# One kernel of causal attention and expert layers: its attention stage and its expert stage put into one program, with two orders of work inside changed

## The chip, the cores and the metric

The kernel runs on one NeuronCore of a Trainium2 chip. The metric is the device time of one execution in microseconds (us), as the median of several runs. The engines named here are TensorE (PE, with PEld for its weight loads), VectorE (DVE), ScalarE (ACT), GpSimd (POOL) and SyncE (SP), which issues most DMAs.

## The reference

A transformer layer over 4096 tokens of width 256 in float32: attention and a feed-forward part with experts both read the same normalised input, and both are added to x.

```python
xn = _layernorm(x)
# attention: 16 heads of 16, causal, over all 4096 tokens
Q, K, V = (heads(xn @ w) for w in (W_Q, W_K, W_V))
probs = softmax(Q @ K.T / 4 + causal)
att = (probs @ V).reshape(B, S, 256) @ W_o
# experts: 16 of them, each takes the C = 512 tokens that score highest for it
scores = softmax(flat_x @ gate_w.T).T
topk_weight, topk_idx = top_k(scores, C)
xg = flat_x[topk_idx]                                   # [16, 512, 256]
h = gelu(xg @ Wg.T) * (xg @ Wu.T)                       # [16, 512, 1024]
eo = (h @ Wd.T) * topk_weight[..., None]
out = zeros_like(flat_x).at[topk_idx].add(eo)
shared = (gelu(xn @ Sg.T) * (xn @ Su.T)) @ Sd.T         # inner width 512
return x + att + out + shared
```

## The kernel before

The program has three blocks. A block is a stretch in which every engine runs its own list of instructions; at its end all engines wait for one another. The first block makes small constants. The second holds the projections (`project`) and the attention (`attend`). The third (`experts`) first runs `mix`, which for 8 groups of 512 tokens computes the output projection of attention and the shared expert and adds x, and then the 16 routed experts in a loop of 8 turns of two.

**Attention.** There are 32 tiles: 4 groups of 4 heads by 8 stretches of 512 queries. For each tile the row maxima of the scores come first ("units": a product of 128 queries by up to 512 keys on PE at L1248, reduced by DVE at L1075). Then come the scores again, transposed and with the maximum taken off (L1337), the exponential on ACT (L1205), and the products with V (pieces, L1364). The order of all this is written out ahead by a planner as a list of rows (`STREAM`); each engine goes through it in its own way.

**Uses.** Units, maxima, the counts of the top-k search, the output rows of a tile ("out") and the late work share four PSUM banks, `a_pm0` to `a_pm3`, in turn. Each such piece of work is a use: PE fills the bank of use n only when DVE has done with use n - 4 (`eng.wait_ge(s_mf, BANKS + DONE[USES[n - BANKS]])`), and DVE counts the uses up in the order in which it does them, so that `DONE` of a use is its place in DVE's order.

**Late products.** The q and k projections of the last two token groups are not made in `project` but among the first rows of attention: two groups of four products of 128 by 512, `late_products` (L467), in rows 2 to 5 and 8 to 11. The float32 result is split in a high part, rounded by ACT (`late_high`, L486), and the rest, which DVE subtracts (`late_low`, L490). `late_low` ends the use. Both parts are then stored by SP (`late_store`). In DVE's order (`TURNS`, made by `delayed`) each late use is put off by `BEHIND = 3` uses: after a late product PE fills the other three banks, and DVE does these three first. `BEHIND` is also used by the planner to place the maximum of a tile behind three units of the next.

**The seam.** At the end of attention PE turns the last tile's rows (`use(("out", LAST))`, L1292, after ACT has copied them from PSUM, L1211), DVE divides them by their sums (L1150, L1152), SP stores them and waits for all stores. After the block's end PE begins `mix` with the turns of the first group's attention rows (`turn(0, 0)`, `turn(0, 1)`, L1600, whose inputs `k.A0` and `k.A1` were loaded during attention), opens the bank of the token lists (`lists.open_pe`, L647), and makes the gate and up products (`up`, L1588). The operand of the first group, `k.XP0`, is made by POOL during attention; that of the second group (`m_xp`) by POOL at L1493 and L1410 from a load that SP issues in `mix`.

**Experts.** For each expert PE makes gate and up products (L1888) and down products (L1898) for 8 chunks of the inner width; the results of the down products for four blocks of 128 tokens, t = 0 to 3, gather in two banks `e_po`, two blocks in each. The last chunk's product ends with `s_dn`. DVE then waits for `s_dn` and scales the four blocks by the tokens' weights (L1868), and POOL, once all four are there, adds them to the output rows with four indirect DMAs (L1763). PE may write `e_po` again when the four are scaled; it asks for that behind the next expert's first two pairs of products. `wait_alone` is a wait followed by an increment of a counter that nothing else uses.

Of the kernel before, what the change touches and what calls it, by code (L numbers as in the profile page):

```python
# [57 lines left out]
class Core:  # L58


    def __init__(self, nc, ctx):
        self.nc, self.ctx = nc, ctx
# [7 lines left out]
    def sem(self, name):  # L70
        return self.ctx.enter_context(self.nc.semaphore(name))
# [631 lines left out]
def attend(nc, k, shared, front, project):  # L703
# [14 lines left out]
    with ctx:  # L718
# [13 lines left out]
        s_kv = [front.s_kv, [c.sem(f"a_kv1{n}") for n in range(NQ)]]  # L732
        s_q = [*front.s_q, *[c.sem(f"a_sq{n}") for n in range(4, SLOTS)]]
        s_nq = [c.sem(f"a_nq{n}") for n in range(SLOTS)]
        s_one, s_pad, s_one1, s_pad1 = front.s_one, front.s_pad, c.sem("a_one1"), c.sem("a_pad1")
        s_mb, s_mf, s_nm, s_sp = (c.sem(f"a_{n}") for n in ("mb", "mf", "snm", "sp"))
        s_st, s_ex, s_pv, s_ev, s_rd = (c.sem(f"a_{n}") for n in ("st", "ex", "pv", "ev", "srd"))
        s_as = [c.sem(f"a_as{n}") for n in range(2)]
        s_shd, s_ws, s_wh, s_wl = (c.sem(f"a_{n}") for n in ("shd", "sws", "wh", "wl"))
# [23 lines left out]
        LAG, BACKLOG, PAUSE, BEHIND = 2, 6 * P, 2, 3  # L763
# [206 lines left out]
        with nc.Block() as block:  # L970
            @block.sync
            def _(eng):
                def fetch_q(t):
                    front.queries(eng, QT[t % SLOTS], s_q[t % SLOTS], *TILES[t])

                def store_rows(t):
                    g, j = TILES[t]
                    eng.wait_ge(s_mf, BANKS + DONE["out", t])
                    eng.dma_start(av[:, j * NB:(j + 1) * NB, g * HG * DH:(g + 1) * HG * DH],
                                  AN[t % 2][:, :, :]).then_inc(s_as[t % 2], 16)  # L980

                project_sync(eng)
                for u in EVENTS:
                    if u[0] == "max":
                        store_max(eng, u[1])
                        if u[1] == 0:
                            front.ahead(eng, 3)
                    elif u[0] == "late":
# [9 lines left out]
                for w in range(len(WINDOWS)):  # L998
                    if w == SOFT + 8:
                        soft.sync(eng)  # L1000
# [70 lines left out]
            def _(eng):  # L1071
# [118 lines left out]
                for u in TAIL:  # L1190
                    work(u)
# [808 lines left out]
```

## Time and profile before

| | us |
|---|---|
| median of 3 runs | 2385.93 |
| lowest, highest | 2378.39, 2398.73 |
| the profiled execution | 2398.66 |
| its span, from the first to the last instruction | 2396.4 |

The profiled execution, busy time of each engine with its share of the span and the number of instructions:

```profile
PE 2320.5 (97%) x20269; PEld 1498.3 (63%) x20275; DVE 1927.1 (80%) x3721; ACT 1493.3 (62%) x2901; POOL 247.4 (10%) x239
```

And in 40 equal slices of 60 us, each digit a busy share in tenths; `PEclk` is the clock that TensorE was granted, in tenths of full speed, where 9 stands for 90% or more:

```profile
PE   7889999999999999999999999998999999999997
DVE  6766999999999999999999999975745666666664
ACT  2213677788888787878887777874224454544443
PEclk9976999999999999999999999999999999999998
```

Projection takes the first two slices, attention goes to about 1640 us, `mix` to 1834, the routed experts to 2380. A matmul on a PE at half clock takes about twice as long, so a busy share of 9 there is less work.

### The profile page before, as it was taken

Reading aid. Unit: us, or ns where it says so; the run is one execution under the profiler, and the core shown is the slowest. Engines: PE = TensorE matmul, PEld = TensorE weight load, DVE = VectorE, ACT = ScalarE, POOL = GpSimd, SP = SyncE. Lnnn points to the kernel's source line nnn. Section 1 sums busy time; section 2 is a strip of 40 time slices with the busy share of each in tenths; the row PEclk is TensorE's granted clock in tenths of the full one; section 3 lists DMA queues with packets and bytes.
Section 4 is the critical chain, followed back from the end, with each engine's and each line's share of the span. In section 5 each row is a group of like instructions: output and inputs, shape, how many; then the busy total and the mean of one; then the engine's idle time right before and its main releaser. Section 6 shows DMA issues by size and latency. Waiting matters only on the chain. (4 is left out here: it accounts for less than half of the span.)

```text
span 2396.4 us, 52700 instructions
## 1 busy us (share of the span) xinstructions
PE 2320.5 (97%) x20269; PEld 1498.3 (63%) x20275; DVE 1927.1 (80%) x3721; ACT 1493.3 (62%) x2901; POOL 247.4 (10%) x239
## 2 busy tenths in 40 slices
PE   7889999999999999999999999998999999999997
PEld 4544555455555555555555555556888888888886
DVE  6766999999999999999999999975745666666664
ACT  2213677788888787878887777874224454544443
POOL 3100000000000000000002000001130332333232
PEclk9976999999999999999999999999999999999998
DMA  7813221002100003300001000001343444444444
GB/s 257 317 54 92 57 48 37 10 11 47 40 7 11 12 19 70 62 14 12 6 11 41 4 2 4 14 23 52 106 160 118 98 136 135 122 101 136 137 110 111
DMA packets 141243, 167.98 MB, mean 70 GB/s; under 512 B 53100, under 2 KB 106860, under 8 KB 140956
## 3 DMA queue, kind: packets, MB, share of 16 engines
q1 hardware_dynamic: 126908, 141.96, 19.0%
q0 software_dynamic: 14128, 23.20, 5.3%
q8 instruction: 137, 2.24, 0.4%
q14 instruction: 70, 0.57, 0.1%
HBM read 117.86 MB, written 48.56 MB: 69 GB/s over the span
## 5 line engine op out<-in xcount | busy, mean ns | idle before, releaser
L1075 DVE TENSOR_REDUCE a_mp<-a_pm 128x1 f32<-128x512 f32 (+3 forms) x2176 | 1295.1, 664 | 88.8 <-PE a_pm L1248 47.3
L1205 ACT ACTIVATE a_p<-a_ps 128x512 f32<-128x512 f32 (+2 forms) x2176 | 1120.8, 587 | 371.8 <-PE a_ps L1337 257.2
L1364 PE MATMUL a_po<-a_p,a_v 128*32 128x384 f32 (+2 forms) x8688 | 614.1, 385 | 0.9
L1248 PE MATMUL a_pm<-a_k,a_qr 48*128 48x512 f32 (+3 forms) x1152 | 410.2, 450 | 22.6 <-DVE p_parts L490 9.1
L1248 PE MATMUL a_pm<-a_k,a_q 48*128 48x512 f32 (+3 forms) x1152 | 408.5, 436 | 4.6
L1337 PE MATMUL a_ps<-a_qr,a_k 50*128 50x512 f32 (+3 forms) x1152 | 386.0, 433 | 2.5 <-DMA a_qr<-a_nb 2.5
L1337 PE MATMUL a_ps<-a_q,a_k 50*128 50x512 f32 (+3 forms) x1152 | 372.3, 422 | 0.8 <-ACT a_p L1205 0.5
L1364 PEld LDWEIGHTS a_po<-a_p,a_v 128*32 128x32 f32 x8688 | 202.2, 109 | 201.9 <-issue 133.7
L1337 PEld LDWEIGHTS a_ps<-a_qr,a_k 50*128 50x128 f32 x1152 | 191.8, 191 | 177.0 <-ACT a_p L1205 145.1
L1337 PEld LDWEIGHTS a_ps<-a_q,a_k 50*128 50x128 f32 x1152 | 185.1, 185 | 186.4 <-ACT a_p L1205 160.8
L1806 ACT ACTIVATE e_g<-e_pg 128x512 f32<-128x512 f32 x128 | 76.5, 598 | 242.4 <-PE e_pu L1888 242.4
L1248 PEld LDWEIGHTS a_pm<-a_k,a_qr 48*128 48x128 f32 x1152 | 190.6, 192 | 55.5 <-DVE a_mp L1075 16.2
L1855 DVE TENSOR_TENSOR e_hf<-e_g,e_pu 128x512 f32<-128x512 f32 x128 | 88.1, 688 | 168.9 <-ACT e_g L1806 154.7
L1248 PEld LDWEIGHTS a_pm<-a_k,a_q 48*128 48x128 f32 x1152 | 188.0, 184 | 28.5 <-DVE a_mp L1075 21.9
L1898 PE MATMUL e_po<-e_wdp,e_hp 128*128 128x256 f32 x1536 | 203.3, 284 | 0.0
L1898 PEld LDWEIGHTS e_po<-e_wdp,e_hp 128*128 128x128 f32 x1536 | 196.5, 191 | 8.2
L1888 PE MATMUL e_pg<-a_qr,e_wgup 128*128 128x512 f32 x768 | 197.5, 392 | 0.0
L1888 PE MATMUL e_pu<-a_qr,e_wgup 128*128 128x512 f32 x768 | 194.9, 389 | 0.0
L1888 PEld LDWEIGHTS e_pu<-a_qr,e_wgup 128*128 128x128 f32 x768 | 144.2, 188 | 30.4
L1888 PEld LDWEIGHTS e_pg<-a_qr,e_wgup 128*128 128x128 f32 x768 | 138.1, 189 | 24.2
L1763 POOL DMA_INDIRECT out<-e_y,e_iy x64 | 104.0, 1624 | 270.3 <-DVE e_y L1868 255.6
L1060 POOL CAST a_k<-a_k 128x1024 fp32r<-128x1024 f32 (+1 forms) x4 | 3.7, 929 | 1099.8 <-DMA a_k<-shared 1099.6
(196 smaller groups left out, 2066.2 us busy)
## 6 DMA issues: line engine op xcount, KB each, us to landing
e_wgu<-in_wg SPq DMA_DIRECT2D x18, 1024.0 KB, 5.4
e_wgu<-in_wu SPq DMA_DIRECT2D x18, 1024.0 KB, 7.8
e_wd<-in_wd SPq DMA_DIRECT2D x18, 1024.0 KB, 10.1
a_k<-k_parts SPq DMA_DIRECT2D x58, 128.0 KB, 3.1
q_parts<-p_parts SPq DMA_DIRECT2D x14, 512.0 KB, 6.4
k_parts<-p_parts SPq DMA_DIRECT2D x14, 512.0 KB, 7.6
a_q<-q_parts SPq DMA_DIRECT2D x96, 64.0 KB, 2.4
a_qr<-q_parts SPq DMA_DIRECT2D x78, 64.0 KB, 2.3
```

What stands on the lines that cost most here:

```text
L1060: eng.tensor_copy(k.WSH[n][:, :, 0, :], k.WSH[n][:, :, 1, :].bitcast(F32)).then_inc(s_wh, 1)
L1075: eng.tensor_reduce(mp[:, i, heads[0]:heads[-1] + 1, r, kc], ps[:, 0:len(heads) * w].rearrange("p (a n) -> p a n", n=w), AX.X, ALU.max).th ...
L1205: eng.activation(pr[:, i, heads[0]:heads[-1] + 1, off:GT], pS[n % HEADS][:, 0:len(heads) * w].rearrange("p (a n) -> p a n", n=w), ACT.Exp) ...
L1248: last = eng.matmul(ps[:, n * w:(n + 1) * w], QT[t % SLOTS][tile, a, r * P:(r + 1) * P], KT[g % 2][tile, a, kc * GT:kc * GT + w], start=n ...
L1337: last = eng.matmul(ps[:, m * w:(m + 1) * w], KT[TILES[t][0] % 2][tile, a, b * P:(b + 1) * P], QT[t % SLOTS][tile, a, off:GT], start=m == ...
L1364: last = eng.matmul(pO[h * VW:(h + 1) * VW, lo:hi], V[TILES[t][0] % 2][:, b, h * VD:h * VD + VW], PR[blk % PBUF][:, h, lo:hi], start=b == ...
L1763: eng.indirect_dma_start(out=rows, out_offset=bass.IndirectOffsetOnAxis(ap=IY[s][:, t:t + 1], axis=0), in_=Y[s][t][:, :], in_offset=None, ...
L1806: eng.activation(G[ic % 2][:, :], pG[ic % 2][:, :], ACT.Gelu).then_inc(s_gl, 1)
L1855: eng.tensor_tensor(HF[ic % 2][:, :], G[ic % 2][:, :], pU[ic % 2][:, :], ALU.mult).then_inc(s_h, 1)
L1888: last = eng.matmul(ps[ic % 2][:, :], WGUP[ic][:, a, w * DC + d, :], XT[s][:, d, b, :], start=n == 0, stop=n == DC * len(PAIRS) - 1)
L1898: last = eng.matmul(pO[t // 2][:, (t % 2) * D:(t % 2 + 1) * D], HP[ic % 4][:, a, t * P:(t + 1) * P], WDP[ic][:, b, :], start=ic == n == 0 ...
```

## The change

Three things are changed.

1. The attention no longer has a block of its own. `attend` returns its five lists of instructions, and `experts` runs them in its block ahead of those of `mix`; the wait of all engines for one another at the seam is gone. The semaphores of `attend` are made to live as long as the program. PE waits instead for DVE's uses (`taken`): for all but the last before `turn(0, 0)`, then it does the last tile's rows, then `turn(0, 1)`, then it waits for DVE's last use before it opens the list bank. SP waits for `k.s_xp0` before it loads the third group's tokens over `k.XT0`.
2. In DVE's order a late use is put off by `HOLD = 1` use instead of three. `BEHIND` stays 3 where the planner uses it.
3. The routed experts' last step goes by halves: a new semaphore `s_do` is raised by the last product of token block 1, DVE starts to scale blocks 0 and 1 at it and waits for `s_dn` only before block 2. POOL waits for each scaled block by itself before its indirect DMA.

The diff without the lines that are only indented differently:

```diff
 class Core:
-        self.nc, self.ctx = nc, ctx
+        self.nc, self.ctx, self.whole = nc, ctx, ctx
     def sem(self, name):
-        return self.ctx.enter_context(self.nc.semaphore(name))
+        return self.whole.enter_context(self.nc.semaphore(name))
...
 def attend(nc, k, shared, front, project):
-        LAG, BACKLOG, PAUSE, BEHIND = 2, 6 * P, 2, 3
+        LAG, BACKLOG, PAUSE, BEHIND, HOLD = 2, 6 * P, 2, 3, 1
...
                     if u[0] == "late":
-                        held.append([u, BEHIND])
+                        held.append([u, HOLD])
...
-        with nc.Block() as block:
-            @block.sync
-            def _(eng):
+        def sync(eng):
...
-                use(("out", LAST))
+            return lambda: use(("out", LAST))
+
+        def taken(eng, before=0):
+            eng.wait_ge(s_mf, BANKS + DONE["out", LAST] - before)
+
+        assert AT["out", LAST] % BANKS
+    return sync, gpsimd, vector, scalar, tensor, taken
...
 def mix(nc, k, x, wo, sg, su, sd, out):
                     if g > 0:
                         eng.wait_ge(s_xl, g)
+                    else:
+                        eng.wait_ge(k.s_xp0, 2)
                     tokens(g + 2)
...
-            for d in range(DC):
-                turn(0, d)
+            taken(eng, 1)
+            turn(0, 0)
+            last_rows()
+            turn(0, 1)
+            taken(eng)
             lists.open_pe(eng, pI)
...
-def experts(nc, k, out, mixed):
+def experts(nc, k, out, attended, mixed):
...
+                attend_sync(eng)
                 mix_sync(eng)
...
+                attend_gpsimd(eng)
                 mix_gpsimd(eng)
...
-                        wait_alone(k, eng, s_oe, TG * (e + 1) + TG)
                         for t in range(TG):
+                            wait_alone(k, eng, s_oe, TG * e + t + 1 + TG)
                             eng.indirect_dma_start(out=rows, out_offset=bass.IndirectOffsetOnAxis(
...
+                attend_scalar(eng)
                 mix_scalar(eng, first)
...
+                attend_vector(eng)
                 mix_vector(eng, first)
...
-                        eng.wait_ge(s_dn, IC * (e + 1) + IC)
                         eng.wait_ge(s_w4, e + 1)
                         eng.wait_ge(s_add, e + 1)
                         for t in range(TG):
+                            if t == 0:
+                                eng.wait_ge(s_do, e + 1)
+                            elif t == 2:
+                                eng.wait_ge(s_dn, IC * (e + 1) + IC)
                             eng.tensor_scalar(Y[s][t][:, :], pO[t // 2][:, (t % 2) * D:(t % 2 + 1) * D],
...
+                        if ic == IC - 1 and t == 1:
+                            last.then_inc(s_do, 1)
                     last.then_inc(s_dn, 1)
...
-                mix_tensor(eng, lambda eng: turn(0, 0, 0))
+                last_rows = attend_tensor(eng)
+                mix_tensor(eng, lambda eng: turn(0, 0, 0), last_rows, taken)
```

## Rows read from the trace of the kernel before

**Rows 1.** Table of stages: stretch, length, busy PE, PEld, DVE, ACT, POOL, PEclk, DMA.

```profile
108.90:231.80 122.90, 104.85 (x545) 52.80 (x546) 73.54 (x131) 33.66 (x64) 2.47 (x5) 0.65 0.25 81
231.80:1639.70 1407.90, 1398.03 (x15006) 747.44 (x15006) 1313.34 (x2415) 1103.71 (x2152) 15.53 (x10) 1.00 0.11 25
...
1834.50:2380.20 545.70, 545.63 (x3176) 481.56 (x3174) 342.39 (x663) 273.66 (x540) 162.14 (x124) 1.00 0.47 129
```

**Rows 2.** PE's waits from 100 to 235 us: total, times, longest.

```profile
PE a_pm L1248 <- DVE p_parts L490: 9.1, 4, 2.5
PE a_pm L1248 <- DVE p_xn L490: 4.7, 2, 2.4
PE a_pm L1248 <- DVE p_x L490: 4.0, 2, 2.3
PE a_ps L1337 <- DMA a_qr<-a_nb: 2.5, 1, 2.5
```

**Rows 3.** Timeline around one late product: start, length, instructions, idle before.

```profile
158.76 1.99 PE L467 MATMUL a_pm<-p_xs,p_wqk 128*128 128x512 f32 x4
...
160.78 0.60 ACT L486 ACTIVATE p_x<-a_pm 128x512 fp32r<-128x512 f32 x1 [1.09 <-PE a_pm L467]
161.21 1.89 DVE L1075 TENSOR_REDUCE a_mp<-a_pm 128x1 f32<-128x512 f32 x3 [0.71 <-PE a_pm L1248]
163.01 0.68 DVE L490 SCALAR_TENSOR_TENSOR p_x<-a_pm,p_x 128x512 fp32r<-128x512 f32 x1
...
163.75 0.79 PE L1248 MATMUL a_pm<-a_k,a_qr 48*128 48x512 f32 x2 [2.34 <-DVE p_x L490]
...
164.58 2.96 DVE L1075 TENSOR_REDUCE a_mp<-a_pm 128x1 f32<-128x512 f32 x5 [0.89 <-PE a_pm L1248]
```

**Rows 4.** Timeline: PE's first instruction behind two other stalls.

```profile
173.58 0.53 PE L1248 MATMUL a_pm<-a_k,a_qr 48*128 48x384 f32 x2 [1.63 <-DVE p_x L490]
...
1311.29 0.49 PE L1248 MATMUL a_pm<-a_k,a_qr 48*128 48x512 f32 x1 [1.77 <-DVE a_mp L1075]
```

**Rows 5.** One microsecond each, behind these two stalls, columns as in rows 1.

```profile
174.00:175.00 1.00, 1.00 (x12) 0.99 (x11) 0.64 (x2) 0.04 (x1) 0.00 (x0) 0.50 0.19 76
...
1312.00:1313.00 1.00, 1.00 (x12) 0.46 (x5) 1.00 (x3) 0.00 (x0) 0.00 (x0) 1.00 0.00 0
```

**Rows 6.** Groups of instructions: the late products (four matmuls each), busy us, mean ns.

```profile
L467 PE MATMUL a_pm<-p_xs,p_wqk 128*128 128x512 f32 x32 | 27.2, 1000 | 0.1
```

**Rows 7.** Two stretches of attention at either clock, columns as in rows 1.

```profile
194.23:231.78 37.55, 37.55 (x250) 19.59 (x252) 23.30 (x39) 16.43 (x31) 2.47 (x5) 0.50 0.37 113
235.19:272.60 37.41, 36.92 (x377) 20.10 (x375) 36.61 (x66) 24.68 (x49) 0.00 (x0) 1.00 0.33 87
```

**Rows 8.** Timeline of the seam between attention and mix.

```profile
1640.45 0.63 PE L1292 MATMUL a_pm<-identf,a_ot 128*128 128x128 f32 x4 [0.80 <-ACT a_ot L1211]
...
1641.41 0.42 DVE L1152 TENSOR_TENSOR a_an<-a_pm,a_rd 128x256 f32<-128x256 f32 x1
...
1645.24 1.08 PE L1600 MATMUL m_pt<-identf,a_qr 128*128 128x128 f32 x4 [4.16 <-PEq L970]
...
1647.05 2.37 PE L1588 MATMUL m_pg<-a_qr,a_k 128*128 128x512 f32 x6
...
1647.88 1.04 POOL L1493 CAST m_xp<-e_wgup 128x1024 fp32r<-128x1024 f32 x1 [84.99 <-DMA e_wgup<-xn_t]
...
1649.25 1.54 PE L1588 MATMUL m_pu<-a_qr,a_k 128*128 128x512 f32 x6
...
1667.38 0.94 PE L1588 MATMUL m_pg<-m_xp,a_k 128*128 128x512 f32 x3
```

**Rows 9.** Timeline of the end of the last expert.

```profile
2375.48 4.65 PE L1898 MATMUL e_po<-e_wdp,e_hp 128*128 128x256 f32 x36
...
2380.17 1.66 DVE L1868 TENSOR_SCALAR e_y<-e_po,e_w 128x256 f32<-128x256 f32 x4 [1.46 <-PE e_po L1898]
2382.67 1.61 POOL L1763 DMA_INDIRECT out<-e_y,e_iy  x1 [16.41 <-DVE e_y L1868]
```

More of the change, by code:

```diff
@@ new lines, in scalar, with exps, rows @@
+        def scalar(eng):
+            def exps(u):
+                _, blk, heads, i = u
+                n, off = NTH[u], skipped(blk)
+                w = GT - off
+                if blk >= PBUF:
+                    eng.wait_ge(s_pv, blk - PBUF + 1)
+                if blk == PBUF - 2:
+                    front.stored(eng)
+                eng.wait_ge(s_st, n + 1)
+                pr = PR[blk % PBUF][:, :, :].rearrange("p (a i) n -> p i a n", i=2)
+                eng.activation(pr[:, i, heads[0]:heads[-1] + 1, off:GT],
+                               pS[n % HEADS][:, 0:len(heads) * w].rearrange("p (a n) -> p a n", n=w),
+                               ACT.Exp).then_inc(s_ex, 1)
+            def rows(t):
+                eng.wait_ge(s_pv, START[t + 1])
+                eng.copy(OT[t % 2][:, :], pO[:, :]).then_inc(s_ev, 1)
+            project_scalar(eng)
+            eng.activation(OT[0][:, 0:1], k.onesf[:, 0:1], ACT.Exp).then_inc(s_ws, 1)
+            eng.wait_ge(s_ws, 1)
+            for w, row in enumerate(STREAM):
+                if w == SOFT + 3:
+                    soft.scalar(eng)
+                for u in row:
+                    if u[0] == "score":
+                        exps(u)
+                    elif u[0] == "late":
+                        eng.wait_ge(s_mb, AT[u] + 1)
+                        front.late_high(eng, *u[1:], pM[AT[u] % BANKS])
+                for t in range(LAST + 1):
+                    if OVER[t] == w:
+                        rows(t)
@@ L1581, in vector, with tensor @@
             ahead(eng, 1)
-        def tensor(eng, ahead):
+        def tensor(eng, ahead, last_rows, taken):
             def product(ps, lhs, rhs, terms, first=True, last=True):
@@ L1685, in experts @@
     IC = IE // P
+    attend_sync, attend_gpsimd, attend_vector, attend_scalar, attend_tensor, taken = attended
     mix_sync, mix_gpsimd, mix_vector, mix_scalar, mix_tensor, mix_banks, mix_sums, mix_stored = mixed
@@ L1962, in program @@
                 first = project(nc, k, x, wq, wk, wv, gate, front)
-                attend(nc, k, (sg, su, sd, wo), front, first)
+                attended = attend(nc, k, (sg, su, sd, wo), front, first)
             k.ctx = inner
@@ L1966, in program @@
             mixed = mix(nc, k, x, wo, sg, su, sd, out)
-            experts(nc, k, out, mixed)
+            experts(nc, k, out, attended, mixed)
 def kernel(**inputs):
```

765 lines of the change are left out of this document (365 added, 400 removed).

## The prediction

> **What bounds the kernel now.** I read the table of stages first, beside it the clock row of the page, then the waits of TensorE (PE), then instructions in order of time. In the long attention stage and in the experts' stage PE is busy all the time: 1398 of 1408 us and 545.6 of 545.7 us, at full clock [rows 1]. Nothing that another engine gains there moves the end. That leaves three places where PE does not work or works slowly. The first is 108.9 to 231.8 us: 122.9 us in which PE works 104.9 and VectorE (DVE) only 73.5, and the mean granted clock is 0.65 [rows 1]; in the page's clock row it is the only low place. Here PE waits 9.1 + 4.7 + 4.0 = 17.8 us in 8 waits for the second parts of the late products (line 490), beside one wait of 2.5 us for a DMA [rows 2]. The second is the hole between the two blocks at 1640 to 1645 us, the third the tail after PE's last matmul at 2380.1 us.
>
> **The change part by part.** The sums stand against the profiled execution, 2398.66 us (span 2396.4 and 2.3 around it). The median of the three runs is 2385.93, the lowest 2378.39; that the profiled one is 12.7 above the median matters below.
>
> *Second parts one use later.* One late product as it is now [rows 3]: PE computes it from 158.76 to 160.75, then fills its other three banks and must have this one back. ScalarE (ACT) makes the first part from 160.78 to 161.38. DVE first reduces the three uses behind it (161.21, 1.89 us, 0.63 each), only then makes the second part (163.01 to 163.69), and PE goes on at 163.75 after 2.34 us of idleness. DVE then is idle for 0.89 itself, since nothing is in a bank. With one use instead of three, DVE does one reduction, to 161.84, and the second part, to 162.5. ACT is done 0.46 us before that one starts, so the new order adds no wait there as long as ACT is idle when the product ends; here it had stood idle for 1.09 us [rows 3]. PE goes on two reductions earlier, 1.26 us; DVE does these two reductions while PE fills the bank. Queued behind the second part on DVE are just these two, and PE needs their banks only after it has filled the freed one. Eight times 1.26, with somewhat less where the reductions are narrow, is 9.8 us if PE is what limits. If DVE limits, only its own idle time behind each second part goes: eight of the size of the 0.89 are 7.1, and with smaller ones among them perhaps 5. I take 9, nearer to the PE end, since DVE works only 60% of this stage; the ends are 5 and 9.8. The stores of the late parts on SyncE's queue start earlier by the same and move past nothing.
>
> *The clock.* The stalls cost more than their own time. After the stall of 1.63 us that ended at 173.58 the granted clock is 0.50, 1.2 GHz; after one of 1.77 us that ended at 1311.29, in the same attention stage, it stays at 1.00, 2.4 GHz [rows 4, 5]. This one, the other seven stalls and the DMA wait were all followed by a fall. With 1.2 us taken from each, the eight are about 1.0 us on the mean (17.8/8 less 1.2), shorter than any that was followed by a fall and than the 1.77 that was not. So I expect that most of these falls go. The first one, after the 2.5 us DMA wait, stays. What the falls cost: the eight products take 27.2 us together where the one at full clock took 1.99 [rows 3, 6], so 27.2 - 15.9 = 11.3 too much, of which some 1.7 (the first) stays: 9.6 to gain. After the last product the clock stays at 0.50 for 37.6 us; DVE does 23.3 us of work in it, which at full clock, where it works 36.6 of 37.4, takes 23.8 [rows 7]: 13.7 to gain. Together 23.3. The bounds: nothing, if every fall comes as before; and at the other end DVE as the limit of the whole stretch, 73.5/0.98 = 75 us for 122.9, so 48 for stalls and clock together.
>
> A rule that speaks against this: the Trainium skill, TensorE: Matmul & The Clock Gate, section A second HAM failure mode: psum-queue depth-cycling, says that a kernel which cycles PSUM banks idles in small steps between groups of matmuls often enough for the clock to swing. By it the falls would go on, the 23.3 would be zero and the time would come out at the first rival's. The trace agrees for the stretch before 231.8 and not behind it: 1408 us of the same four banks run at 1.00 [rows 1].
>
> *One program.* Now PE ends its last piece at 1639.65, the transposes of the last rows at 1641.08, DVE the rows at 1641.83; then all engines wait for the last store and the block's end, PE starts again at 1645.24 with its transposes slow (1.08 us for what took 0.63), then the first gate product at 1647.05, 2.37 us at the low clock against 1.54 for six of the same shape behind it, and the next at 1649.25 [rows 8]. In the new order the four transposes of the first turn fill the time in which ACT copies, then come the last rows' four and the second turn's: three times some 0.62 from 1639.7, so 1641.6. The new wait of PE is for DVE's rows, 0.3 + 0.42 us behind the last rows' transposes: 1641.8. With the opening matmul the first gate product starts at 1642.0 and, at full clock, the next at 1643.4, 5.8 us earlier. Is anything late then? ACT's casts and its table load end before 1643.6, gelu needs both products, about 1645. POOL's first operand of the second group comes from a load that SyncE issues behind the last store as before, and is cast from 1647.9 as before, with the subtraction behind it, to about 1651.5. PE asks for it 5.8 us earlier, at 1661.6 instead of 1667.4: still 10 us of cover. The added wait on SyncE for the first group's parts is met long before (POOL has been idle for 85 us at 1647.9 [rows 8]). Behind it DVE and PE take turns as the bound, and both start earlier by the same. Ends: 4.2 (the idle time alone) and 6.5 (all slow instructions too); I take 5.8.
>
> *Experts by halves.* Within the loop PE is full, so 15 of 16 are hidden: DVE's four scalings lie beside the next expert's first products, and PE needs the bank only behind two of them, some 5.5 us. If that cover went, it would be 1.66 us a turn. At the end it counts: 36 matmuls in 4.65 us put the end of the second token block 6 matmuls, 0.7 us, ahead of 2380.13. DVE's first scaling ends at 2379.9 instead of all four at 2381.83, and POOL's first scatter starts 0.84 us behind that, as now [rows 9]: 1.9 us earlier. The four scatters follow one another on POOL and each gets its own wait and increment; that costs between 0 and three times 0.84. The waits are met by then, so I take 0.4: 1.5 us net, ends -0.6 and 1.9.
>
> **Sum.** 9 + 5.8 + 1.5 = 16.3 us without the clock, 39.6 with it: 2398.66 - 39.6 = 2359.1.
>
> **The rivals.**
> 1. *The falls go on.* For it: a stall of 1 us is left at each product, the free banks are as few, and the first fall comes before the first product anyway. Against it: the idle time of 1.77 us with no fall [rows 4, 5]. Then the median moves by 16.3 alone: 2369.6; with the profiled run's luck 2382.
> 2. *A new wait for ACT.* If ACT has exponentials before the first part, DVE waits for it and holds two reductions back. For it: only 0.46 us of margin. Against: ACT's idle time before these products. At 0.6 us (one exponential) for each of 8 the gain shrinks by 4.8: about 2364 with the clock's gain.
> 3. *Slower.* The clock needs longer to rise after the last product. It stayed low for 37.6 us there although PE had no idle time, so what ends it is not plain. Each us of it costs 1 - 23.8/37.6 = 0.37 us [rows 7]. From 44 us more on it eats the 16.3, and from 109 us more the kernel is over 1% slower, about 2410. Nothing speaks for so much, as the stall before it gets shorter.
> 4. *The hole stays.* The store and PE's wait could still meet at the seam, if some operand of the mix stage comes late. Then 5.8 is missing: 2365.
>
> **How the numbers follow.** One per cent, 23.9 us, is about what a measurement of this kernel can tell from no change, with runs that lie 20 us apart. Forecast 0.53: 2359, its own range 2345 to 2367. First rival 0.32, 2362 to 2382; the second 0.06, the fourth 0.05, the third 0.04. The median already holds some clock luck that the profiled run lacks (12.7 us, nearly the 13.7 of the stretch behind the last product); so the gain over the median is 27 and not 39.6. Low end 2343: all of the 48 us, 5.8 and 1.5. High end 2379: the first rival with most of the bad luck. Faster by over 1% means below 2362: most of the forecast's chance and a little of the others, 0.53; within 1%: 0.43; slower: 0.04.
>
> **What would show it.** In the changed profile: PE's waits on line 490 near 9 us instead of 17.8; DVE's second part behind one reduction; the clock of 108.9 to about 200 us above 0.85, and no stretch at 0.50 behind the last product. From the last piece of attention to the first gate product 2.4 us instead of 7.4. The first scatter about 0.5 us behind PE's end instead of 2.5. The forecast is wrong if the clock row keeps its two low digits: then 2370. It is also wrong if the stage comes out bound by something unseen here, such as the loads that follow the late stores.

## The result, and the profile after

The changed kernel takes 2378.70 us (median of 20 runs, 2371.90 to 2387.39). The kernel before, in 20 runs beside it, takes 2399.74 us (2378.39 to 2403.47). The ratio is 0.9931, with a 95% interval from 0.9915 to 0.9947: 0.7% faster, some 16.5 us; the difference of the two medians is 21.0. Forecast were 2359.1 us, faster by more than 1%, with a range of its own from 2345 to 2367; the median lies outside it, in the range of the first rival (2362 to 2382). The three runs of before that stood ahead of the prediction (median 2385.93) were on the low side of the 20. The profiled one, 2398.66, is what before mostly takes.

The page of the changed kernel, in the parts that answer to those shown of before (busy time and share of the span, then tenths of busy time and of the granted clock in 40 slices of 59.5 us):

```profile
PE 2319.7 (97%) x20275; PEld 1497.4 (63%) x20275; DVE 1928.6 (81%) x3721; ACT 1493.0 (63%) x2901; POOL 251.3 (11%) x239
...
PE   7989999999999999999999999999999999999997
...
DVE  6767999999999998999999999875745666666664
...
PEclk9976999999999999999999999999999999999998
```

The clock row keeps its two low digits, the third and the fourth slice. That was the sign named for the forecast being wrong. The profiled run took 2383.5 us (span 2381.8), 15.2 less than the profiled run of before. It is one of the slower executions of the changed kernel: 16 of its 20 runs took less. Cut into four stretches, the two spans differ as follows (attention: first score product to the end of the last piece; seam: from there to the first up product of the mix stage; tail: from PE's last matmul to the end of the span):

| us | before | after | difference | forecast |
|---|---|---|---|---|
| ahead of attention | 107.65 | 108.31 | +0.66 | 0 |
| attention | 1532.01 | 1517.49 | -14.52 | -32.3 (9 stalls, 23.3 clock) |
| seam | 9.59 | 3.93 | -5.66 | -5.8 |
| mix and experts | 730.88 | 737.33 | +6.45 | 0 |
| tail | 16.3 | 14.7 | -1.6 | -1.5 |

Seam and tail came as forecast, and attention is 17.8 us short of the forecast. The mix stage gave back what the seam had brought.

**Attention.** The first late product as it runs now (timeline of the changed kernel; start, duration, engine, line, what it does; in brackets the idle time before it and who ended it):

```profile
109.51 3.48 PE L467 MATMUL a_pm<-p_xs,p_wqk 128*128 128x512 f32 x4
...
113.60 0.69 DVE L1071 TENSOR_REDUCE a_mp<-a_pm 128x1 f32<-128x512 f32 x1 [2.86 <-PE a_pm L1242]
...
114.21 0.68 DVE L490 SCALAR_TENSOR_TENSOR p_parts<-a_pm,p_parts 128x512 fp32r<-128x512 f32 x1
...
114.94 0.50 PE L1242 MATMUL a_pm<-a_k,a_qr 48*128 48x512 f32 x2 [1.14 <-DVE p_parts L490]
```

The second part follows one reduction where in [rows 3] it followed three, and PE is idle for 1.14 us and not 2.34. PE's waits in 100 to 235 us, in the groups that answer to [rows 2] (engine and line waited for: us in total, times, longest):

```profile
PE a_pm L1242 <- DVE p_parts L490: 4.5, 4, 1.3
...
PE a_pm L1242 <- DVE p_xn L490: 1.9, 2, 1.0
...
PE a_pm L1242 <- DVE p_x L490: 1.6, 2, 1.1
```

The wait for the DMA is 2.5 us as before. The eight waits on line 490 are 4.5 + 1.9 + 1.6 = 8.0 us instead of 17.8. The 9.8 us that went are the upper end of my bounds. Then the same stage in the table of stretches (from:to, length, busy time and count of PE, PEld, DVE, ACT, POOL; mean granted clock, DMA share, GB/s), whole and in part:

```profile
108.90:231.80 122.90, 114.52 (x699) 57.51 (x698) 86.83 (x159) 43.17 (x82) 2.46 (x5) 0.72 0.28 90
...
174.00:226.00 52.00, 50.92 (x359) 26.16 (x361) 34.97 (x61) 22.67 (x44) 2.46 (x5) 0.60 0.35 102
```

The mean clock rose from 0.65 [rows 1] to 0.72 only. The eight stalls are now 0.43 to 1.32 us long. Six of them, and the DMA wait, are still followed by a fall of the clock within 3 us; of the other two, one comes while the clock is low already, and behind the one of 1.14 us at 138.8 the clock stays up. The last fall is even longer than before, about 44 us at the low clock (171.3 to 215.7) instead of 37.6. It comes behind a stall of 0.96 us, and the last product already runs in it:

```profile
170.27 0.50 PE L1242 MATMUL a_pm<-a_k,a_qr 48*128 48x512 f32 x1 [0.96 <-DVE p_xn L490]
...
173.02 3.78 PE L467 MATMUL a_pm<-p_xs,p_wqk 128*128 128x512 f32 x4
```

```profile
171.30:215.70 44.40, 43.45 (x260) 21.58 (x259) 28.62 (x49) 18.60 (x35) 2.46 (x5) 0.50 0.35 108
```

The product takes 3.78 us where 1.99 is full clock [rows 3].

**Seam and mix stage.** PE's order at the seam, where before it was idle for 4.16 us [rows 8]:

```profile
1624.94 0.86 PE L1358 MATMUL a_po<-a_p,a_v 128*32 128x256 f32 x16
1625.82 0.66 PE L1603 MATMUL m_pt<-identf,a_qr 128*128 128x128 f32 x4
...
1628.27 1.62 PE L1591 MATMUL m_pg<-a_qr,a_k 128*128 128x512 f32 x6
```

The mix stage's first transposes now stand ahead of the last rows' transposes, and the gate product starts 2.5 us behind the last piece, at full clock, where it was 7.4 at the low one. But 20 us on, PE waits for something that it did not wait for before:

```profile
1635.52 1.66 POOL L1495 CAST m_xp<-e_wgup 128x1024 fp32r<-128x1024 f32 x1 [86.98 <-DMA e_wgup<-xn_t]
...
1636.19 1.06 DVE L658 TENSOR_SCALAR l_ohi<-l_one,r_pcol 128x256 bf16<-128x256 bf16 x1
...
1637.26 2.46 POOL L1410 TENSOR_TENSOR m_xp<-e_wgup,m_xp 128x1024 fp32r<-128x1024 f32 x1
...
1638.74 1.52 DVE L1410 TENSOR_TENSOR m_hp<-m_hf,m_hp 128x512 fp32r<-128x512 f32 x1 [0.69 <-ACT m_hp L1514]
...
1644.78 1.04 POOL L1495 CAST a_qr<-a_qr 128x1024 fp32r<-128x1024 f32 x1 [5.07 <-PE m_pu L1591]
1644.81 1.28 DVE L653 TENSOR_TENSOR l_one<-r_iota,r_run 128x256 bf16<-128x256 f32 x1
...
1645.90 2.40 POOL L1410 TENSOR_TENSOR a_qr<-a_qr 128x1024 fp32r<-128x1024 f32 x1
1646.02 2.83 DVE L655 TENSOR_TENSOR l_olo<-r_iota,scores 128x512 bf16<-128x512 f32 x1
...
1651.32 1.09 PE L1603 MATMUL m_pt<-identf,a_k 128*128 128x128 f32 x4 [4.71 <-DVE m_at L1410]
```

POOL makes the split operands of two groups (line 1495 and the subtraction of line 1410). Each of its four instructions has one of DVE's beside it that takes longer than its like: 1.06 for 0.28, 1.52 for 0.69, 1.28 for 0.41 and 2.83 for 0.68 (the like of the last stands 3.5 us later, at 1649.49). That is 4.6 us of DVE's time. DVE gets to the operand of PE's transpose that much later, and PE waits 4.7 us; before, this wait was 0.9 us. The clock falls in this wait, and the next gate product takes 2.91 us for 1.54. The clock is low from 1649.3 to 1656.1, and once more for 3.4 us from 1714.1, behind another wait.

Only the first pair of POOL's instructions has changed its place in the stage. The second pair starts 15.05 us behind the first up product in both kernels. In the kernel before it drew out one row by 0.78 us and one by 0.2:

```profile
1664.30 1.67 POOL L1493 CAST a_qr<-a_qr 128x1024 fp32r<-128x1024 f32 x1 [12.90 <-PE m_pu L1588]
...
1664.99 1.06 DVE L658 TENSOR_SCALAR l_ohi<-l_one,r_pcol 128x256 bf16<-128x256 bf16 x1
```

The first pair had put DVE's rows back by 1.6 us, and so the second pair met others of them, for another 3.0 us.

### The profile page after: what moved, and what is told of

The parts are those of the page before. It is cut to its first block, busy times and chain, and to the rows that moved or that the text cites. A ratio compares the mean times of both kernels' runs of the same rounds, so it can differ in the third digit from the quotient of the medians.

```text
span 2381.8 us, 52791 instructions
## 1 busy us (share of the span) xinstructions
PE 2319.7 (97%) x20275; PEld 1497.4 (63%) x20275; DVE 1928.6 (81%) x3721; ACT 1493.0 (63%) x2901; POOL 251.3 (11%) x239
## 4 chain that ended last, share of the span: by engine, by line
PE 73%; DVE 24%; issue 1%; ACT 1%; DMA 0%; POOL 0%; SPq 0%; DVEq 0%; POOLq 0%; ACTq 0%
DVE a_mp L1071 20%; PE a_po L1358 15%; PE a_ps L1331 13%; PE e_po L1912 8%; PE e_pg L1902 7%; PE e_pu L1902 7%; PE a_pm L1242 7%; PE m_po L1591 2%; PE a_pm L1254 2%; PE a_ps L1343 2%; PE p_pq L446 2%; PE m_pg L1591 1%; PE m_pu L1591 1%; PE a_pm L467 1%; PE p_pv L436 1%
## 5 line engine op out<-in xcount | busy, mean ns | idle before, releaser
L1331 PEld LDWEIGHTS a_ps<-a_q,a_k 50*128 50x128 f32 x1152 | 185.1, 185 | 186.4 <-ACT a_p L1200 161.0
```

The source lines that it names most:

```text
L1331: last = eng.matmul(ps[:, m * w:(m + 1) * w], KT[TILES[t][0] % 2][tile, a, b * P:(b + 1) * P], QT[t % SLOTS][tile, a, off:GT], start=m == ...
```

## The experiments

The first four kernels are seen beside the kernel before in the same batch (2400.21 us, 13 runs); the batch of the next four has 2399.79 for it (23 runs), that of the last two 2399.78 (17 runs). Since these and the 2399.74 of the result agree to 0.5 us, kernels of different batches are compared by their medians. Where stages of a run are named, they are those of its one profiled execution.

**hold_only.** The kernel before, with nothing but the shorter hold:

```diff
-            held.append([u, BEHIND])
+            held.append([u, 1])
```

> The kernel before with only the late products' second parts one use later instead of three. Theory A: nearly all of the measured gain comes from here, since the stalls shrink by 9.8 us (17.8 to 8.0) and the clock gives a few us more: 12 to 16 us faster than before (ratio 0.994 to 0.995). Rival B: the three parts simply add up as forecast, 9 here, 5.8 at the seam and 1.5 at the end: 9 us faster (0.996), and TensorE's clock between 109 and 232 us no higher than the 0.65 of before.

Measured: 2374.28 us (4 runs, 2369.51 to 2381.89), ratio 0.9907 [0.9871, 0.9942]. PE's stalls are 8.2 us, as in the changed kernel. The median is 25.9 us below before, more than both expectations had it, and even 4.4 below the changed kernel, which has two more changes; the intervals of the two ratios overlap, and so do the runs. So this part alone brings nearly all of the gain, and the rest of the change nothing that can be told from the spread. Attention took 1500.6 us in the profiled run, 16.9 less than in the changed kernel, with the same order of work there. What differs is the clock, in its table of stretches:

```profile
108.90:231.80 122.90, 112.83 (x859) 58.57 (x857) 99.21 (x182) 51.19 (x101) 2.47 (x5) 0.89 0.33 102
...
170.00:208.00 38.00, 34.40 (x326) 18.41 (x325) 34.74 (x62) 21.09 (x43) 2.47 (x5) 1.00 0.44 135
```

In 170 to 208 us DVE does 34.74 us of work in 38.0 us at full clock. In the changed kernel's row above, from 174 to 226, it needs 52.0 us at 0.60 for 34.97. So a low stretch behind the last product costs 14.0 us, which is the 13.7 of my step. The price was right. Whether it is paid varies between executions whose stalls are the same: short falls, six of them, are there in this run's stage too, and only the long one is missing.

**program_only.** The changed kernel with the hold back at three uses and the experts' halves undone, so one program alone:

```diff
-        LAG, BACKLOG, PAUSE, BEHIND, HOLD = 2, 6 * P, 2, 3, 1
+        LAG, BACKLOG, PAUSE, BEHIND, HOLD = 2, 6 * P, 2, 3, 3
...
```

> The changed kernel with the late parts three uses later again and the experts' last step whole again, so that only the block's end between attention and mix is gone. Theory A: the seam (last piece to second product of mix) is 5.7 us shorter, but GpSimd's split of the second group's tokens now falls beside VectorE's list rows and holds them up, and the mix stage is 5 to 6.5 us longer: the whole is within 1.5 us of before (0.9995 to 1.0005). Rival B: the longer mix stage of the profiled execution was an accident of its clock: 5 to 6 us faster (0.9977), mix as long as before (730.9 us from its second product to the last matmul).

Measured: 2397.62 us (10 runs), ratio 0.9993 [0.9964, 1.0022]. The seam took 3.9 us instead of 9.6, and the stage behind it 736.7 instead of 730.9. The edit brings 5.7 us and gives 5.8 back, as the first of the two expectations had it; alone it is worth nothing that can be measured. Attention stayed as before (17.8 us of stalls, clock 0.65).

**early_second.** The changed kernel, but the second group's load is issued inside attention, and POOL splits it behind the last piece instead of behind the load (`k.second` issues the load that `tokens(1)` issued in the mix stage):

```diff
+                if w == OVER[LAST - 2] + 2:
+                    eng.wait_ge(s_pv, START[LAST - 1])
+                    k.second(eng)
...
+        k.pieces_over = lambda eng: eng.wait_ge(s_pv, START[LAST + 1])
...
-            tokens(1)
...
                 if g > 1:
                     eng.wait_ge(s_gu, IC * (g - 1))
+                else:
+                    k.pieces_over(eng)
```

> The changed kernel, with the load of the second group's tokens issued on SyncE's queue during attention, right behind the pieces of the last tile but one, instead of behind the last store; GpSimd splits them as soon as attention's last piece is done. Same work, one load moved. Theory A (GpSimd beside VectorE): GpSimd's two instructions lie beside VectorE's work on PSUM at the seam, no VectorE instruction of mix is stretched by more than 1 us, TensorE's wait of 4.7 us for m_at is gone, mix is 730 to 732 us again and the whole 5 to 7 us faster than the changed kernel (0.9905 of before). Rival B: the wait has another cause, such as the clock: no faster than the changed kernel (0.993), mix 735 us or more.

Measured: 2367.43 us (4 runs, 2366.08 to 2371.79), ratio 0.9872 [0.9843, 0.9901]. POOL's instructions in the timeline, and the one of DVE's lists that is drawn out:

```profile
1613.88 1.04 POOL L1506 CAST m_xp<-e_wgup 128x1024 fp32r<-128x1024 f32 x1 [76.72 <-PE a_po L1361]
...
1632.74 1.66 POOL L1506 CAST a_qr<-a_qr 128x1024 fp32r<-128x1024 f32 x1 [15.38 <-PE m_pu L1602]
...
1633.42 1.06 DVE L658 TENSOR_SCALAR l_ohi<-l_one,r_pcol 128x256 bf16<-128x256 bf16 x1
```

The first pair is over before DVE's lists begin. Of the second, only one of DVE's is drawn out by 0.78 us and one by 0.2, as in the kernel before. PE's wait for m_at is 0.9 us again.

The stages behind the seam took 733.9 us, 3.4 less than in the changed kernel and 3.0 more than before; the rest is two short falls of the clock in the mix stage. The median gained 11.3 us on the changed kernel, more than the 5 to 7 expected and more than this edit can be worth there. Attention, which it hardly touches, was 1506.1 us in the profiled run instead of 1517.5. From 100 to 235 us the clock fell three times only (at 108.2, 121.9 and 162.8), the last time for 44 us, a row of the table of stretches:

```profile
162.80:207.20 44.40, 43.45 (x260) 21.43 (x260) 28.49 (x48) 18.61 (x35) 2.47 (x5) 0.50 0.35 107
```

PE is busy for 43.45 of 44.40 us in this stretch. Its only wait is the one of 0.95 us that ends at 170.2; behind that PE works without a gap for 36.9 us and stays at 0.50, 1.2 GHz.

**fill.** The changed kernel with four matmuls of zeros near each stall. PE does them ahead of the third use behind each late product, in that use's own bank, which is free by then; the use behind it is the one for which PE would wait. The use overwrites the zeros:

```diff
+        FILL = 4
...
+                        n = AT[u]
+                        if n >= 3 and USES[n - 3][0] == "late":
+                            eng.wait_ge(s_mf, BANKS + DONE[USES[n - BANKS]])
+                            eng.wait_ge(soft.s_io, 1)
+                            for _ in range(FILL):
+                                eng.matmul(pM[n % BANKS][:, :], k.ZB[:, 0:P], k.ZB[:, :], start=True, stop=True,
+                                           skip_group_check=True)
                         use(u)
```

> The changed kernel with four more matmuls of zeros (bf16, 512 columns) in front of the third unit behind each late product, into that unit's own free bank, so that TensorE works through part of the time in which it would stall; their results are overwritten. They cost nothing where the stall of 0.9 to 1.3 us covers them (0.9 us at full clock, 1.7 at half). Theory A: the falls of the clock come from the stalls, so with the stalls filled the clock stays at 1.00 from the first product on, the products take 2.0 instead of 3.6 us and the 44 us at 0.50 behind the last one go: 10 to 20 us faster than the changed kernel. Rival B: what keeps the clock low is the kind of work there and not the idle time: the clock falls as before and the kernel is 0 to 5 us slower than the changed one.

Measured: 2359.13 us (4 runs, 2356.00 to 2363.20), ratio 0.9830 [0.9801, 0.9859], 19.6 us below the changed kernel. The first expectation came, near its upper end. Nothing of the computation is shorter by the zeros; PE has almost no pause left, and more matmuls to do. Its timeline at one late product, the table of stretches, and its waits in 100 to 235 us:

```profile
157.51 1.98 PE L467 MATMUL a_pm<-p_xs,p_wqk 128*128 128x512 f32 x4
...
160.62 0.81 PE L1394 MATMUL a_pm<-r_zb 128*128 128x512 bf16 x3 [0.16 <-issue]
```

```profile
108.90:231.80 122.90, 118.44 (x913) 61.33 (x916) 103.52 (x188) 54.55 (x107) 2.47 (x5) 0.93 0.34 107
```

```profile
PE a_ps L1332 <- DMA a_qr<-a_nb: 5.2, 2, 2.7
PE a_pm L1243 <- DVE p_parts L490: 0.2, 1, 0.2
```

Only 0.2 us of the waits on line 490 is left; the waits for the DMA are now two, 5.2 us together. The products run at 1.98 us and the mean clock is 0.93. Behind the first fall, which the first wait for a DMA brings (110.0 to 113.4), none comes until the second such wait (2.7 us, it ends at 183.5), and the low stretch behind it, from 185.1, is 13.7 us. Attention is 1496.5 us, 35.5 less than before. If 9.8 of it are the stalls' own time, as in the changed kernel, 25.7 are left for the clock, where my step had 23.3.

**fill_before.** The same with eight matmuls in the kernel before, whose order stays:

> The kernel before (second parts three uses later, stalls of 2.2 us on the mean) with eight matmuls of zeros (bf16, 512 columns) in front of the third unit behind each late product, 1.7 us at full clock. The order on VectorE and the time from a product to its second part stay as before; only TensorE is not idle in between. Theory A: the idle time makes the clock fall, and the clock was worth more than the stalls themselves: the clock of 109 to 232 us is above 0.85, and the kernel is 15 to 30 us faster than before (0.988 to 0.994), though nothing else is sooner. Rival B: the clock follows the kind of work: no rise, and 0 to 10 us slower than before, as the fillers take 3.4 us at half clock.

Measured: 2390.15 us (10 runs), ratio 0.9972 [0.9946, 0.9998]. Its clock in 108.9 to 231.8 us is 0.85 instead of 0.65 (table of stretches):

```profile
108.90:231.80 122.90, 109.14 (x693) 53.35 (x694) 80.05 (x144) 37.61 (x73) 2.47 (x5) 0.85 0.28 89
```

Eight of them filled only part of each stall: 11.2 us of idle time are left (5.4 + 3.0 + 2.8), so short falls stay. The gain, 9.6 us, is less than the 15 I expected at the least. The order of the work is the old one, so I put this gain down to the clock alone. The clock is worth less as long as the old order sets the pace: here the mean clock of the stage is 0.20 higher than before and attention 10.0 us shorter; between the changed kernel and fill it is 0.21 higher, and attention is 21.0 us shorter.

**lift.** The changed kernel with sixteen matmuls of zeros, once, eight uses behind the last late product:

```diff
+                        if n == AT["late", NG - 1, 3] + 8:
+                            eng.wait_ge(s_mf, BANKS + DONE[USES[n - BANKS]])
+                            eng.wait_ge(soft.s_io, 1)
+                            for _ in range(16):
+                                eng.matmul(pM[n % BANKS][:, :], k.ZB[:, 0:P], k.ZB[:, :], start=True, stop=True,
+                                           skip_group_check=True)
```

> The changed kernel with sixteen matmuls of zeros (bf16, 512 columns; 3.4 us at full clock, 6.9 at half) once, in front of the eighth use behind the last late product, where the clock stays at 0.50 for 44 us in the profiled execution. The stalls are as in the changed kernel. If a dense stretch is what the clock needs to rise there, the low stretch ends behind them, within some 10 us of the last product: 44 us at 0.37 us each are 16, less the 3 to 7 of the fillers and less what runs already had by luck: 3 to 10 us faster than the changed kernel (0.989 to 0.992 of before). If the clock does not answer to it: 3 to 7 us slower than the changed kernel (0.995 to 0.996).

Measured: 2371.83 us (8 runs, 2365.14 to 2376.71), ratio 0.9899 [0.9868, 0.9930], 6.9 us below the changed kernel. PE's timeline at the sixteen:

```profile
183.98 4.82 PE L1393 MATMUL a_pm<-r_zb 128*128 128x512 bf16 x16
188.73 0.50 PE L1242 MATMUL a_pm<-a_k,a_qr 48*128 48x512 f32 x2
```

The fall is there, with the product at 3.78 us, as in the changed kernel, and a stall of 0.95 us behind it. But the low stretch lasts 13.7 us instead of 44 (172.8 to 186.4) and ends amid the sixteen: the score product right behind them takes 0.50 again. What the 4.8 us of extra work cost is in the 6.9. That the sixteen ended it is not shown by this one profile, since the low stretch of fill was as short without them, and hold_only has no long one at all. What speaks for it is that all eight runs are below the changed kernel's median; the intervals of the two ratios overlap.

**hold_zero.** The changed kernel with the second part directly behind its product, ahead of even the one reduction:

```diff
-            held.append([u, HOLD])
+            out[-1].append(u)
```

> The changed kernel with the second part made at once, ahead of the next use instead of behind it. VectorE then waits for ScalarE's first part: it comes 0.7 us behind the product's end, so TensorE goes on at 1.4 us behind it instead of 1.87, and the stall is 0.65 instead of 1.0 us: 8 times 0.45 are 3.6 us. Theory A (the clock answers to the idle time): the shorter stalls also mean fewer falls than the five of the changed kernel, 5 to 12 us faster than it (0.988 to 0.991 of before). Rival B: VectorE's new wait for ScalarE eats the gain: within 3 us of the changed kernel (0.992 to 0.994).

Measured: 2376.65 us (10 runs, 2368.04 to 2403.25), ratio 0.9928 [0.9892, 0.9964]. The stalls shrink to 4.6 us, 3.4 less, and the median by 2.1, within the spread, as the second expectation had it. The clock of the stage was 0.79 in the profiled run. What of the stalls is left is enough for falls: one of its runs took 2403 us at a mean clock of 0.969, lower than the 0.976 that is the lowest on record for before. Over the whole execution, the mean clock in the median of the runs is 0.978 before, 0.983 in the changed kernel, between 0.984 and 0.985 here, and 0.994 in fill. So shorter stalls buy a little of the clock, absent ones most of it.

**pool_late.** The kernel before, its seam untouched, but POOL's split of the second group is held until two up products of the first are done, so that it falls beside DVE's lists, as in the changed kernel:

```diff
-            if g > 1:
-                eng.wait_ge(s_gu, IC * (g - 1))
+            eng.wait_ge(s_gu, IC * (g - 1) if g > 1 else 2)
```

> The kernel before with one wait more: GpSimd splits the second group's tokens only when the second pair of products of mix is done, some 4 us into mix, instead of at its very start. The operand is still ready 8 us before TensorE asks for it. If GpSimd beside VectorE's list rows is what made the mix stage of the changed kernel longer, it happens here too, without any change at the seam: VectorE's l_one, l_olo, l_ohi and m_hp instructions are stretched by 2 to 5 us together, and mix is 2 to 6 us longer than the 730.9 of before. If the cause is another one, mix stays at 730 to 733.

Measured: one run, 2387.12 us. The stages behind the seam took 738.0 us instead of 730.9, with the hole of the seam still there (10.1 us). The timeline of POOL and DVE:

```profile
1634.83 1.18 POOL L1492 CAST m_xp<-e_wgup 128x1024 fp32r<-128x1024 f32 x1 [91.78 <-PE m_pu L1587]
...
1635.03 1.53 DVE L655 TENSOR_TENSOR l_olo<-r_iota,scores 128x512 bf16<-128x512 f32 x1
...
1636.48 2.43 DVE L658 TENSOR_SCALAR l_ohi<-l_one,r_pcol 128x256 bf16<-128x256 bf16 x1
```

PE's wait for m_at behind the seam is 5.3 us. POOL's second pair draws out another row by 2.1 us. So POOL's place alone makes the loss. The whole run was still 12.7 us below the batch's median of before, because its attention took 1513.0 us and not 1532.0: with 17.8 us of stalls as ever, but a clock of 0.87 in this stage. Nothing there had been changed. This is how much one execution says about the clock.

**program_early.** One program alone with the moved load (program_only and early_second):

> Only the block's end taken away, and the second group's load moved into attention; late parts three uses later and the experts' last step whole, as before. Without the moved load this edit gave nothing (0.9993). If GpSimd's work beside VectorE's list rows is what took the gain of the seam, it is there now: seam 3.9 us instead of 9.6, TensorE's wait for m_at 0.9 instead of 4.7, mix 731 to 734 us, 3 to 6 us faster than before (0.9975 to 0.9988). If not, the ratio stays at 0.999 to 1.000.

Measured: 2392.03 us (10 runs), ratio 0.9954 [0.9929, 0.9980], where program_only had 0.9993. The stages behind the seam took 730.86 us, the seam 3.9. Together that is 5.7 us less than before. With the collision gone, nothing is given back. By the medians it is 7.8 us below before, more than the 3 to 6 expected, and 5.6 below program_only, though the two intervals overlap.

**fill_early.** The changed kernel with the fill and the moved load:

> Both edits that helped: the changed kernel with the stalls behind the late products filled (four matmuls of zeros) and the second group's load moved into attention. If they are independent, the sum holds: fill was 19.6 us below the changed kernel's median of 2378.7, and the moved load takes 3.5 to 7 us off the mix stage. Expected 2352 to 2356 us, ratio 0.980 to 0.982 of before. If the moved load were good only through the clock of attention, nothing would be added to fill: 2359.

Measured: 2355.06 us (6 runs, 2349.16 to 2377.46), ratio 0.9836 [0.9802, 0.9871]. Attention took 1490.3 us and the stages behind the seam 730.90. PE's wait behind the seam is 0.9 us. The attention stage's row in the table of stretches:

```profile
108.90:231.80 122.90, 120.68 (x978) 63.15 (x977) 109.60 (x200) 59.28 (x116) 2.47 (x5) 0.99 0.35 110
```

Here the stage has its full clock, and DVE works 109.6 of 122.9 us. It is the lowest median of all kernels run, inside the 2352 to 2356 expected, 4.1 us below fill; the intervals of the two ratios overlap. Its run of 2377 us, at a mean clock of 0.982, shows that the clock can still fall.

## Why the prediction was wrong, point by point

**The stalls, 9 us: right.** They went from 17.8 to 8.0, 9.8 us, in the changed kernel and to 8.2 in hold_only. PE set the pace. The second rival, a new wait for ACT, would have kept 4.8 us of them and did not come.

**The clock, 23.3 us: this step failed.** The profiled pair gives 14.5 - 9.8 = 4.7 us. The medians, 21.0 us apart, leave 21.0 - 9.8 - 0.8 = 10.4, the ratio's 16.5 leave 5.9 (0.8 is what seam, mix stage and tail bring together). So the step brought a fifth of what it was to bring, or by the medians less than half. The failed sentence is "shorter than any that was followed by a fall and than the 1.77 that was not. So I expect that most of these falls go". Six of the eight shorter stalls were followed by a fall. The evidence for a harmless length was one row, of 1.77 us at 1311 [rows 4, 5], from another place and from one execution. That row was luck. The changed kernel has the same wait at the same place of the program, and there a fall follows it:

```profile
1296.21 0.50 PE L1242 MATMUL a_pm<-a_k,a_qr 48*128 48x512 f32 x1 [1.76 <-DVE a_mp L1071]
```

```profile
1297.70:1301.10 3.40, 3.40 (x26) 1.87 (x25) 2.65 (x6) 1.57 (x3) 0.00 (x0) 0.50 0.00 0
```

In pool_late a fall follows it too (1.78 us), in program_early none does (1.64 us). The mix stage shows the same: PE waits there twice for 1.8 us in each of the 12 profiles, and 8 of these 24 waits are followed by a fall, none of them in the profile of before, three of them in those of the changed kernel and early_second. So one profile without a fall does not make a length of stall harmless.

The rest of the step held, as far as the runs show. The falls go with the stalls: fill leaves almost none of the stalls on line 490, and most falls are gone. The price held too: 14.0 us for the long low stretch instead of 13.7, and 25.7 in all in fill instead of 23.3. What I had expected of a shorter stall came only with none. The rule of the Trainium skill that I had set against the step (TensorE: Matmul & The Clock Gate, A second HAM failure mode: psum-queue depth-cycling) had it right for this stage: with the small waits for a bank still there, the swings go on. That nothing at all would be gained, as I had reckoned from it, was too little, by the 4.7 to 10.4 us above.

**The seam, 5.8 us: right, and given back.** It was 5.7. The failed sentence is "Behind it DVE and PE take turns as the bound, and both start earlier by the same". POOL does not start earlier by the same. Its load is issued behind the last store. SyncE's queue has it in the changed kernel at

```profile
1631.95 0.35 SPq L1456 DMA_DIRECT2D e_wgup<-xn_t  x1
```

and in the kernel before at

```profile
1644.31 0.36 SPq L1456 DMA_DIRECT2D e_wgup<-xn_t  x1
```

That was 2.7 us ahead of the first gate product (1647.05), and now it is 3.7 us behind it (1628.27). Even counted from the last piece of attention the load comes 1.5 us later than before, since SP waits for the last store, and this wait took 2.5 us instead of 0.5. POOL's pair lay ahead of DVE's lists (it ended at 1651.4, and the first list row began at 1653.45); now it lies beside the lists. I had asked whether POOL's operand is in time for PE, which it was, and not whose work it runs beside. That was 3.8 us of PE's wait (4.7 for 0.9), and with the two low stretches of the clock in this stage 6.5. pool_late makes this loss with the seam untouched, early_second, program_early and fill_early take the wait back to 0.9.

**The halves, 1.5 us net: right.** The tail is 14.7 us for 16.3. The first scatter starts 0.75 us behind PE's end instead of 2.5:

```profile
2366.49 1.66 DVE L1882 TENSOR_SCALAR e_y<-e_po,e_w 128x256 f32<-128x256 f32 x4 [0.84 <-PE e_po L1912]
...
2367.81 1.61 POOL L1772 DMA_INDIRECT out<-e_y,e_iy  x1 [15.87 <-DVE e_y L1882]
```

The scatters are 0.30 us apart, as before, so their waits of their own cost nothing that can be seen. No run has this part alone, but the tail goes with it in every profile: it is 14.5 to 14.8 us in the five other kernels that have the halves and 16.3 to 16.4 in the five that do not.

**The sum and its base.** Without the clock it was 16.3 us, and 9.8 + 5.7 - 6.5 + 1.6 = 10.6 came. The first rival (the falls go on) had said 2382 "with the profiled run's luck", and the profiled run is 2383.5: two errors, 4.7 that the clock brought and 6.5 that POOL cost, nearly cancel. The base was wrong as well: the forecast set off from the profiled run in its sum but let the median of three runs set the gain that counts, and that median lies 13.8 below the one of 20.

**What stays open.** What beside idle time makes the clock fall or come back was not settled: why nearly every wait among the late products is followed by a fall and only one in three of the longer ones in the mix stage, and why a low stretch lasts 13.7 us in one run and 44 in the next with PE as busy. It may be how dense the matmuls around it are; lift suggests this, but no run separates it from chance. Fill does two things at once, it takes PE's idle time away and gives it more matmuls, and no run tells which of the two keeps the clock up. The first fall, behind the wait of 2.5 us for a DMA, was left as it is.

## What to carry to other kernels

Where PE idles in small steps and the granted clock is below 1.00, do not count on the clock when you make the steps shorter: here halving them took away their own time and less than half of what the low clock cost. Filling them with matmuls that nobody needs brought back most of it; see in the table of stretches whether it stays at 1.00. A stall that was not followed by a fall in one profile may be followed by one in the next, so look for the same stall in several. When a wait is removed, ask of every engine that starts at another time not only whether it is in time, but whose instructions it now runs beside. And take the base of a forecast from many runs: with a clock that falls by chance, three runs can lie 14 us beside the median.

## What the runs showed of the hardware

**POOL and DVE block each other for whole instructions.** A row of DVE that takes 0.68 us alone took 2.83 beside POOL's subtraction of 2.40 and ended 0.55 us behind it, as if it had run only then; 0.41 became 1.28 beside the cast of 1.04. It goes the other way too: the cast at 1635.52, begun while DVE was busy with its lists, took 1.66 us for 1.04. DVE's instructions that read PSUM were not touched: m_hf from m_pu took 0.68 us at 1637.37, inside POOL's 2.46. The Trainium skill (SBUF — State Buffer, Who interferes with whom, and the section SBUF: two separate sides) says that the two share a pair of ports as an exclusive lock: whichever starts first has it for its whole instruction, where DVE has two inputs in SBUF or runs in a two-port mode. The trace agrees in the four rows and in the one from PSUM.

**PE can stay at 1.2 GHz while it is busy.** It did so for 36.9 us without a gap at 0.50 (early_second, 170.3 to 207.2) and for 37.6 in the kernel before [rows 7]. In lift such a stretch ended amid 16 matmuls of zeros. Such a stretch came behind a wait of PE each time; what is computed afterwards may have a say in how long it lasts, but that is not shown.

**The same stall is followed by a fall of the clock in one execution and not in another.** A wait of 1.6 to 1.8 us at one place of attention was followed by one in two of the four profiles that have it, and waits of 1.8 us in the mix stage in 8 cases of 24.

**The same code differs by 19 us between executions.** The kernel before took 2381.31 to 2403.60 us in 13 runs on one chip, and its attention 1532.0 us in one profile and 1513.0 in that of pool_late, all of it in the clock of one stage (0.65 and 0.87).
